# Half of the row-wise scales of a Mamba scan on GpSimd instead of ScalarE

## What is computed

```python
dt = jax.nn.softplus(jnp.einsum('blr,dr->bld', dt, dtw) + dtb)
A = -jnp.exp(A_log)
def step(h, inp):
    u_t, dt_t, B_t, C_t = inp
    dA = jnp.exp(dt_t[:, :, None] * A)
    h = h * dA + (dt_t * u_t)[:, :, None] * B_t[:, None, :]
    y = jnp.einsum('bds,bs->bd', h, C_t)
    return (h, y)
```

## Time and profile before

| | |
|---|---|
| median of 3 runs | 3762.82 us |
| profiled execution | 3769.06 us |
| its span, first to last instruction | 3767.3 us |
| VectorE (DVE) busy | 3295.3 us, 87% |
| TensorE (PE) busy | 2766.6 us, 73% |
| GpSimd (POOL) busy | 2711.5 us, 72% |
| ScalarE (ACT) busy | 2696.5 us, 72% |
| mean granted TensorE clock | 0.872 of full speed |
| first scan to last scan (the loop) | 46.9 to 3437.1 us |

### The profile page before, as it was taken

How to read it: one execution, slowest core, us unless ns; L and a number is a source line. 1 busy time by engine, 2 the same in 40 slices (tenths; PEclk the granted TensorE clock), 3 DMA queues, 4 the chain that set the end, 5 groups by cost and what they waited for, 6 DMA issues and landing times.

```text
span 3767.3 us, 51199 instructions
## 1 busy us (share of the span) xinstructions
PE 2766.6 (73%) x17178; PEld 2347.0 (62%) x17178; DVE 3295.3 (87%) x3315; ACT 2696.5 (72%) x6280; POOL 2711.5 (72%) x1335
## 2 busy tenths in 40 slices
PE   5677676766677677787777777887777687878775
PEld 3556555655556567676666666776666576767654
DVE  5999999999999999998999999998999999995100
ACT  6768686877878687877878597877868688764221
POOL 5878787878877787877778688777878787664000
PEclk7878887888888899988998799988988798999998
DMA  2231111111111224232321223223321232344664
GB/s 95 74 122 64 45 43 47 44 42 48 46 45 41 82 79 135 85 97 93 96 75 54 101 88 126 83 87 98 97 66 46 93 99 96 103 138 134 203 202 154
DMA packets 159451, 336.20 MB, mean 89 GB/s; under 512 B 27578, under 2 KB 45763, under 8 KB 158548
## 3 DMA queue, kind: packets, MB, share of 16 engines
q1 hardware_dynamic: 155234, 322.15, 26.3%
q0 software_dynamic: 3072, 8.39, 0.7%
q10 hardware_dynamic: 882, 2.38, 0.2%
HBM read 302.05 MB, written 30.80 MB: 88 GB/s over the span
## 4 chain that ended last, share of the span: by engine, by line
DVE 34%; issue 22%; POOL 16%; PE 11%; ACT 10%; DMA 6%; SPq 1%; POOLq 0%; DVEq 0%
DVE h L1073 21%; POOL hC L833 13%; DVE psX L1063 11%; ACT dA L1041 4%; PE psG L1283 3%; DMA w_down<-in_w_exp 3%; DMA w_up<-in_w_exp 2%; PE psY L1331 2%; PE psX L1315 2%; ACT xs L1016 2%; PE psG L1358 1%; PE psX L1358 1%; PE psX L1283 1%; POOL scratch L749 1%; DMA xg<-x_slots 1%
## 5 line engine op out<-in xcount | busy, mean ns | idle before, releaser
L833 POOL TENSOR_TENSOR hC<-h,cb 128x1024 f32<-128x1024 f32 x1024 | 2409.0, 2365 | 715.9 <-DVE h L1073 703.6
L1073 DVE TENSOR_TENSOR_SCAN h<-dA,psX 128x512 f32<-128x512 f32 x2048 | 2367.0, 1205 | 74.7 <-PE psX L1315 48.2
L1041 ACT ACTIVATE dA<-dt,negA 128x255 f32<-128x255 f32 x4096 | 1720.9, 500 | 338.0 <-DVE h L1073 335.1
L1331 PE MATMUL psY<-ident,hC 128*128 128x128 f32 x8192 | 1254.1, 304 | 39.8 <-DVE gT L1087 37.9
L1331 PEld LDWEIGHTS psY<-ident,hC 128*128 128x128 f32 x8192 | 1097.9, 160 | 83.4 <-DVE gT L1087 41.5
L1063 DVE TENSOR_TENSOR psX<-dtu,psX 128x1024 f32<-128x1024 f32 x692 | 836.3, 1209 | 80.2 <-PE psX L1306 41.0
L1315 PE MATMUL psX<-ident,xs 128*128 128x128 f32 x2656 | 443.0, 322 | 345.4 <-DVE h L1073 244.0
L1315 PEld LDWEIGHTS psX<-ident,xs 128*128 128x128 f32 x2656 | 362.4, 166 | 426.1 <-issue 268.7
L1016 ACT ACTIVATE xs<-dtuT,bT 128x512 f32<-128x512 f32 x664 | 441.1, 716 | 0.1
L1306 PE MATMUL psX<-bparts,sel 96*128 96x256 bf16 x692 | 209.4, 303 | 247.7 <-DVE h L1073 239.9
L1283 PE MATMUL psG<-xgT,w_up 128*128 128x128 f32 x1680 | 249.6, 296 | 68.9 <-DMA w_up<-in_w_exp 28.9
(11 more groups left out here) (203 smaller groups left out, 1972.8 us busy)
## 6 DMA issues: line engine op xcount, KB each, us to landing
cb<-c_dram SPq DMA_DIRECT2D x256, 512.0 KB, 3.8
w_up<-in_w_exp SPq DMA_DIRECT2D x268, 256.0 KB, 3.1
w_down<-in_w_exp SPq DMA_DIRECT2D x268, 256.0 KB, 3.0
xg<-x_slots SPq DMA_DIRECT2D x67, 128.0 KB, 3.0
y_slots<-yg SPq DMA_DIRECT2D x67, 128.0 KB, 2.9
x_slots<-got SPq DMA_DIRECT2D x16, 512.0 KB, 5.7
y_slots<-got SPq DMA_DIRECT2D x8, 512.0 KB, 5.7
xin<-in_xT SPq DMA_DIRECT2D x8, 256.0 KB, 4.0
```

What stands on the lines that cost most here:

```text
L833: eng.tensor_tensor(hC[i % NHC][:, :, :], h[i % NH][:, :, :], cw.to_broadcast([P, KI, L]), ALU.mult).then_inc(times_c, 1)
L1041: made = eng.activation(dA[j % NA][:, c, 1:L], dt[n % 2][:, c, 1:L], ACT.Exp, scale=negA[:, JOBS[n][0], c, s:s + 1])
L1073: eng.tensor_tensor_scan(h[i % NH][:, 2 * f:2 * f + 2, :].rearrange("p c t -> p (c t)"), dA[i % NA][:, 2 * f:2 * f + 2, :].rearrange("p c ...
L1331: made = eng.matmul(psY[:, tc, c * P:(c + 1) * P], hC[i % NHC][:, c, tc * P:(tc + 1) * P], ident[:, :], start=s == 0 and c == 0, stop=Fals ...
```

## The change

Three things: the first turned step of each job (s = 2) becomes plain; every second turned step, counted over all jobs from the second on, has its rows scaled by GpSimd and not by ScalarE; GpSimd does this right after hC of the step three before (EARLY), and signals on a semaphore of its own. TensorE waits for the one or the other. The planner's clocks are changed to match, so that all small pieces are placed anew.

```diff
 def is_turned(i):
-    return i % S % 3 == 2 and i > 12
+    return i % S % 3 == 2 and i % S > 2 and i > 12
...
+BY_POOL = {i for i in TURNED if TURNED_TO[i] % 2 == 1}
+POOL_TO = [sum(t < i for t in BY_POOL) for i in range(STEPS + 1)]
+EARLY = 3
...
-SUM, SPREAD, OUTER, SCALE = 1060, 280, 1060, 1340
+SUM, SPREAD, OUTER, SCALE, POOL_SCALE = 1060, 280, 1060, 1340, 1300
...
         def decay(i):
             if i < STEPS:
-                if is_turned(i):
+                if is_turned(i) and i not in BY_POOL:
...
                 at["POOL"] = c_end[i] = max(at["POOL"], scan_end[i], sum_end.get(i - NHC, never)) + 2380
+                if i + EARLY in BY_POOL:
+                    at["POOL"] = scaled[i + EARLY] = at["POOL"] + POOL_SCALE
...
+            def scale_row(i):
+                n, s, at = i // S, i % S, TURNED_TO[i]
+                on.wait_ge(x_in, TURNED[at - 1] + 1)
+                k, filling = turn["dtu_turn", n, KL - 1]
+                on.wait_ge(free[k], filling + 1)
+                for tc in range(KL):
+                    made = eng.tensor_scalar(xs[:, tc, :], dtuT[n % 2][:, tc, :], bT[n % 2][:, tc, s:s + 1], None, ALU.mult)
+                made.then_inc(pool_scaled, 1)
...
                 eng.tensor_tensor(hC[i % NHC][:, :, :], h[i % NH][:, :, :], cw.to_broadcast([P, KI, L]),
                                   ALU.mult).then_inc(times_c, 1)
+                if i + EARLY in BY_POOL:
+                    scale_row(i + EARLY)
                 small_work(plan.beside[i])
...
-                    if is_turned(j):
+                    if is_turned(j) and j not in BY_POOL:
                         scale_row(j)
...
             def turn_x(i):
-                at = TURNED_TO[i]
-                on.wait_ge(scaled, at + 1)
+                if i in BY_POOL:
+                    on.wait_ge(pool_scaled, POOL_TO[i] + 1)
+                else:
+                    on.wait_ge(scaled, TURNED_TO[i] - POOL_TO[i] + 1)
                 on.wait_ge(scanned, 2 * (i - 1))
```

More of the change, by code:

```diff
@@ L558, in decoder_block @@
         decay, times_b, scanned, times_c, summed = sem("decay"), sem("times_b"), sem("scanned"), sem("times_c"), sem("summed")
-        x_in, scaled, y_done, gated = sem("x_in"), sem("scaled"), sem("y_done"), sem("gated")
+        x_in, y_done, gated = sem("x_in"), sem("y_done"), sem("gated")
+        scaled, pool_scaled = sem("scaled"), sem("pool_scaled")
         tapped_by, tap_added, silued = sem("tapped_by"), sem("tap_added"), sem("silued")
```

## The result

The changed kernel takes **3949.87 us** (median of 4 runs, 3939.52 to 3955.09) against 3763.48 us (4 runs, 3762.05 to 3765.62): ratio 1.0487, 95% interval 1.0466 to 1.0509. It is 186 us slower. The forecast was 3777 us with a range of 3750 to 3804: the sign was right, the size was not. The profiled execution took 3939.52 us, with a span of 3937.7 us and a granted clock of 0.856 (before: 0.872).

What follows compares the result with a forecast made beforehand. The prediction took VectorE's scan loop as the bound. Its terms, 18.6 - 10 + 5 + 0 = +13.6 us, gave 3782.7 us for the profiled execution and 3777 us for the median, with a range of 3750 to 3804.

Steps and rivals of the forecast that it cites:

- Part 1: Fewer turned steps: 15 steps get their VectorE product back at 1.24 us each, 18.6 us more with nothing to hide it.
- Part 2: ScalarE loses the scales of 158 more steps, shortening VectorE's waits for transposes: -10 us, bounds 0 and -48.2.
- Part 3: GpSimd gains 158 pairs of 128x512 scales at 1.5 us a pair; some rows come late: +5 us, bounds 0 and 77.
- Rival D: GpSimd's pair costs 2.55 us, making rows late in some 50 places: 77 us in place of 5, 3849 us; chance 0.07.
- Rival E: GpSimd and VectorE disturb each other; near 4010 us if GpSimd's added 237 us held VectorE up in full; chance 0.02.
- Part 5: Planner places small work anew, moving expert tiles into or behind the loop: effects cancel, 0, bounds plus and minus 25 us.
- rival A: GpSimd's slots: sends slip, one or two tiles more follow the loop: 3789 to 3802 us; chance 0.17.
- B: Faster: ScalarE's freed room pulls two tiles or more into the loop: 3752 us, or 3739 with one more; chance 0.22.
- Rival C: VectorE's waits were mostly ScalarE's doing; some 15 us more come back and the loop breaks even: 3763 us; chance 0.07.

Runs made afterwards that it cites:

- experiment 2: Kernel before with s = 2 of jobs 1 to 15 plain, every small piece kept where it stood before: 3801.49 us, ratio 1.0084.
- experiment 3: Changed kernel with its plan kept, but ScalarE makes all 317 rows and GpSimd none: 3821.49 us, ratio 1.0136.
- experiment 4: As experiment 3, but GpSimd also makes its 158 pairs of scales into an hC buffer that is overwritten next: 3917.66 us, ratio 1.0397.
- experiment 6: Kernel before, its plan and 332 turned steps kept, with GpSimd scaling the rows of 158 of them as pairs: 3932.90 us, ratio 1.0430.
- Experiment 5: Changed kernel with EARLY = 5 in place of 3, so GpSimd makes each row two steps sooner: 3945.04 us, ratio 1.0461.
- experiment 8: Changed kernel with one GpSimd product of 128x1024 by broadcast B in place of each pair of scales: 3861.70 us, ratio 1.0240.
- experiment 10: Kernel before plus probes after its loop, timing GpSimd's instruction forms alone and beside VectorE's; ran once, no kernel time read.
- experiment 7: As experiment 6, with one GpSimd product of 128x1024 by broadcast B in place of each pair of scales: 3835.11 us, ratio 1.0171.
- experiment 9: Changed kernel with the planner's pair price 3130 ns, not 1300, and GpSimd's small-piece limit 1800 ns, not 600: 3908.04 us, ratio 1.0375.
- experiment 1: Kernel before with s = 2 of jobs 1 to 15 plain, small pieces placed anew, ScalarE scaling every row: 3824.15 us, ratio 1.0136.

## Why the forecast was wrong

One way from before to the changed kernel leads over three experiments: the gate and the plain steps +32 (experiment 2), the placing +20 (3 less 2), GpSimd's occupation +98 (4 less 3), and +34 from there to the changed kernel. That these add up proves nothing, since each is the difference of two neighbours. What is shown is that the pairs make 132 us of it (the changed kernel less 3), or 162 in before's plan (experiment 6), and that they do it without a late row as well (experiments 4 and 5). How the 132 us divide into late rows, late hC and holds is not shown. In VectorE's own time, the changed kernel's loop has 118 us of waits, 19 us of products and 29 us of holds more than before's.

- **Part 1, 15 products, 18.6 us.** Right as a count and a price (707 products, 1210 ns). The sentence "with nothing to hide it" looked at VectorE alone. What the product delays at the job's start is the gate, which TensorE waits for, and that gave 13 us more. Nor did VectorE wait "almost nowhere" there: 22 us of its idle time before the change stood ahead of steps 4 and 5 of the jobs.
- **Part 2, -10 us.** No run shows it. Wherever rows left ScalarE, VectorE waited longer for transposes than the 48.2 us of before. Only in the changed kernel's plan, with a product of 1.90 us, it waited less than with all rows on ScalarE (54.7 us in experiment 8, 61.6 in experiment 3). No run took ScalarE's scales away with nothing in their place, so that a small gain of this sort stays open.
- **Part 3 is the step that failed.** Its price, 1.5 us a pair with bounds of 0.95 and 2.55, was mis-sized by a factor of two: 3.13 us. Its cost to the kernel, +5 us with a bound of 77, was 132 us. The argument was "one operand to read in place of two halves the second part". Experiment 10 shows the order the other way round: 1564 ns with one full operand and a scalar, 1262 with two full operands. The upper bound fell with it, since it was taken from the product as if no simpler-looking instruction could be slower. The Trainium skill's 769 ns ("GPSIMD Engine Reference", "Elementwise — side-by-side cycle accounting") for a tight loop over 512 elements is not what this instruction reaches in any run here. The second half of the part, "a lag below some 3 us reaches nobody", fails too. It fails for the row, which is due some 1 us after a pair of 1.5 us would end, and for hC: in experiment 4 TensorE waited in 141 places for an hC that had begun less than 3 us late. And with 1.90 us, inside the bounds, the work cost 64 us in before's plan (experiment 7), most of it by holds that no part of the sum had.
- **Rival D came nearest, and under-priced it.** It said that a pair of 2.55 us would end at the limit and make 50 rows late for 77 us, 3849. With 3.13 us TensorE waited for a row 114 times. Its chance of 0.07 rested on the false upper bound. It saw late rows alone. Experiment 5 has none and takes as long: what the kernels with pairs share is the lag of GpSimd, whichever of its products passes it on. With the true price the sum for six steps (18.8 us on GpSimd against 18.4 on VectorE) would have warned of it.
- **Rival E was dismissed by the scans, which indeed did not change** (1180 to 1223 ns, before 1180 to 1222). It did not look at VectorE's small instructions, whose two operands, or one with a scalar, are both in SBUF. They took 29 us more in the loop. So E as priced (near 4010) is refuted, and about a sixth of the loss is its mechanism all the same; in experiments 7 and 8 it is the larger part. The Trainium skill says as much: "GPSIMD Engine Reference", "Key points", names contention with VectorE instructions that have two SBUF inputs, and "SBUF — State Buffer", "Who interferes with whom", adds that the first to issue keeps the shared ports for its whole instruction. Beside GpSimd's products experiment 10 agrees in both directions, 176 to 2264 ns on VectorE and 2337 to 2880 ns on GpSimd. Beside GpSimd's scale by a scalar the traces don't agree: VectorE's instruction took 776 ns where 1.51 us were left. The prediction used the rule for the large instructions only.
- **Part 5, placing, 0 with bounds of 25 us.** In the tail it held: 23 stores after the loop, as before, so rivals A and B both fell. But placing costs some 20 us within the loop (experiment 3), and with pairs in it the planner's price and limit are worth 42 (experiment 9). Without the pairs' price (experiment 1) one tile more did follow the loop, as in rival A. The prediction looked for the cost of placing in the number of tiles only.
- **Rival C** asked for a loop as long as before, and the loop is 180 us longer.

## What to carry to other kernels

Price an instruction that a trace does not have by nothing but a measurement of that very form. An operand less to read is no reason for it to be cheaper, and the widest bound belongs where the sum is most sensitive. Before work is moved to an engine with idle time, add up its work for one period against the bound engine's period: here 18.8 us stood against 18.4 us, which the mean busy share of 72% hid. That is a warning and no safe side: with 1.90 us the sum is 17.6, and the kernel still lost 64 us. Ask too which small instructions of the bound engine lie in the other's idle gaps, for they can be held once the gaps are filled. And look first at the bound engine's own terms, for the same turned steps, used for 48 products fewer, gave 26 us where the move lost 186.

## What the runs showed of the hardware that was not expected

- GpSimd multiplies 512 elements by a scalar in 1.56 us (by a constant 1.49), slower than by a second tensor (1.26) or by a broadcast column (1.04). For 1024 elements the broadcast product takes 1.90 us, against 3.13 for two scales, and the plain hC product 2.34 to 2.37.
- A VectorE product of 16 elements took up to 2.26 us in place of 0.18, until a GpSimd instruction ended; in turn a GpSimd product took 2.88 in place of 2.34. With one operand in PSUM VectorE showed nothing of it.
- The hold depended on GpSimd's instruction: a VectorE scale of 128x256 begun 0.1 us into a GpSimd scale by a scalar took 776 ns with 1.51 us of it left, and 1980 ns when begun 0.1 us into a GpSimd product with 1.83 us left.
- In one job, behind a wait of 4.13 us at the gate in place of 1.48, TensorE's granted clock was 0.50 where it had been 0.98, and the eight matmuls took 1.97 us in place of 1.10.
